# Final norm of an encoder moved into the feed-forward loop, and one GpSimd memset moved later

## The reference

```
out1 = _layernorm(x + attn_out, ln1_g, ln1_b)
h = jax.nn.elu(out1 @ W1 + b1)
ffn_out = h @ W2 + b2
return _layernorm(out1 + ffn_out, ln2_g, ln2_b)      # rsqrt(var + 1e-6) * g + b
```

## Time and profile before

| what | us |
|---|---|
| median of 3 runs | 2630.42 |
| lowest and highest | 2629.88, 2640.3 |
| the profiled execution | 2632.62 |
| its span in the profile | 2630.4 |

### The profile page before, as it was taken

The page is one execution under the profiler, slowest core; times in us unless marked ns, Lnnn a source line. Parts: engine busy times, 40 slices in busy tenths (PEclk is TensorE's granted clock), DMA queues, the critical chain, the costliest instruction groups (busy, mean ns, idle before and its releaser), DMA issues. The chain is left out here.

```text
span 2630.4 us, 95467 instructions
## 1 busy us (share of the span) xinstructions
PE 2416.6 (92%) x39473; PEld 2073.5 (79%) x39473; DVE 1644.4 (63%) x3145; ACT 1457.2 (55%) x4096; POOL 1051.6 (40%) x1152
## 2 busy tenths in 40 slices
PE   6899999999989999997579998999999989899999
PEld 5788888888867888885479986777777778788888
DVE  4566666666667777675655554777777757544553
ACT  3555555555566676664644443777777734422222
POOL 2343344333440000002344444666666623355555
PEclk8999999999999999998869998999999989799999
DMA  5544333334333111110020000200010010065463
GB/s 199 213 152 144 144 144 144 144 144 148 118 150 148 48 40 48 40 40 2 3 69 1 0 0 19 54 26 28 24 30 24 19 53 0 2 139 116 107 134 76
DMA packets 60306, 206.08 MB, mean 78 GB/s; under 512 B 6670, under 2 KB 20498, under 8 KB 51226
## 3 DMA queue, kind: packets, MB, share of 16 engines
q1 hardware_dynamic: 60188, 204.41, 24.5%
HBM read 182.88 MB, written 21.51 MB: 78 GB/s over the span
## 5 line engine op out<-in xcount | busy, mean ns | idle before, releaser
L558 POOL TENSOR_TENSOR l_pn<-l_probs,l_rden 128x1024 f32<-128x1024 f32 x128 | 242.9, 1898 | 454.1 <-DVE l_rden L400 454.1
L494 ACT ACTIVATE l_probs<-ps,l_nmax 128x257 f32<-128x257 f32 x512 | 236.3, 474 | 272.4 <-DVE l_nmax L394 270.2
L959 POOL TENSOR_TENSOR l_probs<-l_probs,l_rden 128x1024 f32<-128x1024 f32 x128 | 242.5, 1895 | 170.5 <-DVE l_rden L810 170.5
L895 ACT ACTIVATE l_probs<-ps,l_nmax 128x257 f32<-128x257 f32 x512 | 236.3, 474 | 59.7 <-DVE l_nmax L804 59.7
L394 DVE TENSOR_REDUCE l_nmax<-ps 128x2 f32<-128x514 f32 x256 | 165.4, 688 | 164.3 <-PE ps L286 164.3
L286 PE MATMUL ps<-l_ctxQ,l_q 32*128 32x257 f32 x3072 | 205.2, 396 | 40.5 <-ACT l_q L501 27.2
L2714 POOL TENSOR_TENSOR m_hh<-m_hh,m_cb 128x512 f32<-128x512 f32 (+1 forms) x136 | 179.7, 1322 | 141.6 <-DVE m_hh L2666 134.4
L804 DVE TENSOR_REDUCE l_nmax<-ps 128x2 f32<-128x514 f32 x256 | 165.4, 688 | 61.1 <-PE ps L696 57.5
L2570 ACT ACTIVATE m_sg<-ps 128x512 f32<-128x512 f32 (+1 forms) x136 | 81.5, 599 | 219.7 <-PE ps L111 218.8
L286 PEld LDWEIGHTS ps<-l_ctxQ,l_q 32*128 32x128 f32 x3072 | 148.6, 186 | 69.0 <-issue 30.7
L2666 DVE TENSOR_TENSOR m_hh<-ps,m_sg 128x512 f32<-128x512 f32 (+1 forms) x136 | 93.9, 690 | 167.6 <-PE ps L111 151.7
(11 more groups left out here) (373 smaller groups left out, 6429.4 us busy)
## 6 DMA issues: line engine op xcount, KB each, us to landing
l_ctxQ<-in_ctx_q SPq DMA_DIRECT2D x32, 1542.0 KB, 6.4
l_ctxK<-in_ctx_k SPq DMA_DIRECT2D x16, 1536.0 KB, 6.4
l_early<-in_ctx_k SPq DMA_DIRECT2D x16, 1536.0 KB
enc_dash<-kept SPq DMA_DIRECT2D x32, 512.0 KB, 3.2
m_cb<-combined SPq DMA_DIRECT2D x32, 512.0 KB, 10.7
l_ctxT<-in_ctx_t SPq DMA_DIRECT2D x32, 385.5 KB, 3.3
m_cb<-combined SPq DMA_DIRECT2D x16, 768.0 KB, 16.6
kept<-enc_va SPq DMA_DIRECT2D x10, 512.0 KB, 2.7
```

Of the source, the lines that this page charges most:

```text
L494: nc.scalar.activation(probs[:, par % 2, hg, :], ps[:, S_B + hg, 0:NK], ACT.Exp, bias=nmax[:, par, hg:hg + 1], accum_out=den[:, par, hg:hg ...
L558: nc.gpsimd.tensor_tensor(pn[:, b % 2, :, :], probs[:, b % 2, :, 0:NK - 1], rden[:, b, :, None].to_broadcast([P, HG, NK - 1]), ALU.mult).t ...
L895: nc.scalar.activation(probs[:, b, hg, :], ps[:, S_B + hg, 0:NK], ACT.Exp, bias=nmax[:, b, hg:hg + 1], accum_out=den[:, b, hg:hg + 1]).the ...
L959: nc.gpsimd.tensor_tensor(pr, pr, rden[:, b, :, None].to_broadcast([P, HG, K_W]), ALU.mult).then_inc(norm_ok, 1)
```

## The change

The block of the final norm is gone. Its work stands in the feed-forward loop, group by group: VectorE computes the variances of a group right after its statistics (`variances`), GpSimd takes them to the power -0.5 and makes the shift (`roots`), ScalarE normalises in the next turn (`final`), GpSimd multiplies by the gain and adds to `k.x` (`added`), and VectorE takes the statistics of x another turn later (`count_x`). The loop has two turns more for it. In the expert stage GpSimd's memset stands behind its eight casts instead of ahead of them.

```diff
             def groups(step):
-                for g in range(NG + 1):
+                for g in range(NG + 3):
                     step(g, g % 2, lambda d: 0 <= g + d < NG)
...
                     for n in range(PART):
                         t = PART * g + n
-                        nc.vector.bn_stats(at(k.stats, t), at(res, t))
+                        last = nc.vector.bn_stats(at(k.stats, t), at(res, t))
+                    last.then_inc(c_ok, 1)
+
+                def variances(g):
+                    ts = slice(PART * g, PART * g + PART)
+                    col = lambda n: k.stats[:, ts, n:n + 1].rearrange("p t o -> p (t o)")
+                    dve.wait_ge(c_ok, g + 1)
+                    if g:
+                        dve.wait_ge(var_ok, g)
+                    nc.vector.tensor_tensor(part[:, 0, :], col(1), col(4), ALU.add)
+                    nc.vector.tensor_tensor(part[:, 1, :], col(1), col(4), ALU.subtract)
+                    nc.vector.tensor_tensor(part[:, 2, :], col(2), col(5), ALU.add).then_inc(p_ok, 1)
+                    dve.wait_ge(p_ok, 2 * g + 1)
+                    nc.vector.tensor_scalar(f_mean[:, ts], part[:, 0, :], -0.5, None, ALU.mult)
+                    nc.vector.tensor_tensor(part[:, 3, :], part[:, 1, :], part[:, 1, :], ALU.mult)
+                    nc.vector.tensor_scalar(part[:, 4, :], part[:, 2, :], 1.0 / D, EPS_ENC, ALU.mult, ALU.add
+                                            ).then_inc(p_ok, 1)
+                    dve.wait_ge(p_ok, 2 * g + 2)
+                    nc.vector.scalar_tensor_tensor(f_var[:, ts], part[:, 3, :], 0.25, part[:, 4, :], ALU.mult, ALU.add
+                                                   ).then_inc(var_ok, 1)
+
+                def count_x(g):
+                    dve.wait_ge(x_ok, g + 1)
+                    nc.vector.nop(nofuse=True)
+                    for n in range(PART):
+                        t = PART * g + n
+                        nc.vector.bn_stats(at(k.stats, t), at(k.x, t))
...
                     if has(-1):
                         result(g - 1, 1 - j)
                         count(g - 1)
+                        variances(g - 1)
+                    if has(-3):
+                        count_x(g - 3)
...
+                def final(g, j):
+                    act.wait_ge(f_ok, g + 1)
+                    if g > 1:
+                        act.wait_ge(x_ok, g - 1)
+                    for n in range(PART):
+                        t = PART * g + n
+                        last = nc.scalar.activation(f4[:, j, n, :], res[:, t, :], ACT.Identity, bias=f_shift[:, t:t + 1],
+                                                    scale=f_rstd[:, t:t + 1])
+                    last.then_inc(fa_ok, 1)
...
                         for c in (2, 3):
                             expo(g, c, True)
+                    if has(-2):
+                        final(g - 2, j)
...
-                        nc.gpsimd.tensor_tensor(xs, xs, rows[:, 4:5, :].to_broadcast(wide), ALU.add)
-
+                        nc.gpsimd.tensor_tensor(xs, xs, rows[:, 4:5, :].to_broadcast(wide), ALU.add).then_inc(xb_ok, 1)
+                    if has(-1):
+                        roots(g - 1)
+                    if has(-2):
+                        added(g - 2, j)
+
+                def roots(g):
+                    ts = slice(PART * g, PART * g + PART)
+                    pool.wait_ge(var_ok, g + 1)
+                    nc.gpsimd.tensor_tensor(f_rstd[:, ts], f_var[:, ts], neg_half[:, :], ALU.pow).then_inc(root_ok, 1)
+                    pool.wait_ge(root_ok, g + 1)
+                    nc.gpsimd.tensor_tensor(f_shift[:, ts], f_mean[:, ts], f_rstd[:, ts], ALU.mult).then_inc(f_ok, 1)
+
+                def added(g, j):
+                    pool.wait_ge(fa_ok, g + 1)
+                    n, xs = f4[:, j, :, :], part_of(k.x, g)
+                    nc.gpsimd.tensor_tensor(n, n, rows[:, 3:4, :].to_broadcast(wide), ALU.mult).then_inc(g_ok, 1)
+                    pool.wait_ge(g_ok, g + 1)
+                    pool.wait_ge(xb_ok, g + 1)
+                    nc.gpsimd.tensor_tensor(xs, n, xs, ALU.add).then_inc(x_ok, 1)
...
-        with ExitStack() as end:
-            sem = lambda n: k.sem(f"fin_{n}")
...
-            @block.scalar
-            def _(act):
-                rstd_act(nc, k, act, ln)
...
-            nc.gpsimd.memset(next_ones, 1.0).then_inc(row_ok, 1)
-            pool.wait_ge(row_ok, 1)
             nc.gpsimd.memset(one[:, :], 1.0).then_inc(one_ok, 1)
...
             for g in range(NG):
                 high(g)
+            pool.wait_ge(xh_ok, NG)
+            nc.gpsimd.memset(next_ones, 1.0).then_inc(row_ok, 1)
+            pool.wait_ge(row_ok, 1)
```

More of the change, by code:

```diff
@@ L1448, in stage_performer @@
             hT = sb("hT", [P, 2, NF, 512])
+            f4, neg_half, part = sb("f4", [P, 2, PART, D]), sb("neg_half", [P, PART]), sb("part", [P, 5, PART])
+            f_mean, f_var, f_rstd, f_shift = [sb(n, [P, T]) for n in ("f_mean", "f_var", "f_rstd", "f_shift")]
+            c_ok, xb_ok, half_set, p_ok, var_ok, root_ok, f_ok, fa_ok, g_ok, x_ok = [sem(n) for n in (
+                "c_ok xb_ok half_set p_ok var_ok root_ok f_ok fa_ok g_ok x_ok").split()]
             (ln, w_mm, set_ok, n_ok, tr_mm, tr_ok, up_mm, low_ok, m_ok, h_ok, y_mm, y_ok, base_ok, sum_ok) = [sem(n) for n in (
@@ L1627, in step @@
                         nc.gpsimd.tensor_tensor(r, r, row[:, None, :].to_broadcast(wide), ALU.add).then_inc(base_ok, 1)
-                        nc.gpsimd.tensor_tensor(xs, xs, rows[:, 4:5, :].to_broadcast(wide), ALU.add)
-                groups(step)
-        with ExitStack() as end:
-            sem = lambda n: k.sem(f"fin_{n}")
-            PART = 4
-            NG = T // PART
-            n4 = end.enter_context(nc.sbuf_tensor("fin_n4", [P, 2, PART, D], F32))
-            shift = end.enter_context(nc.sbuf_tensor("fin_shift", [P, T], F32))
-            ln, sh_ok, n_ok, g_ok, x_ok = sem("ln"), sem("sh_ok"), sem("n_ok"), sem("g_ok"), sem("x_ok")
-            block = end.enter_context(nc.Block())
-            @block.scalar
-            def _(act):
-                rstd_act(nc, k, act, ln)
-                act.wait_ge(sh_ok, 1)
-                for g in range(NG):
-                    if g > 1:
-                        act.wait_ge(x_ok, g - 1)
-                    for n in range(PART):
-                        t = PART * g + n
-                        last = nc.scalar.activation(n4[:, g % 2, n, :], res[:, t, :], ACT.Identity, bias=shift[:, t:t + 1],
-                                                    scale=k.rstd[:, t:t + 1])
-                    last.then_inc(n_ok, 1)
-            @block.gpsimd
-            def _(pool):
-                for g in range(NG):
-                    pool.wait_ge(n_ok, g + 1)
-                    n = n4[:, g % 2, :, :]
-                    nc.gpsimd.tensor_tensor(n, n, rows[:, 3:4, :].to_broadcast([P, PART, D]), ALU.mult).then_inc(g_ok, 1)
-            @block.vector
-            def _(dve):
-                rstd_dve(nc, k, dve, ln, EPS_ENC)
-                nc.vector.scalar_tensor_tensor(shift[:, :], k.mean[:, :], -1.0, k.rstd[:, :], ALU.mult,
-                                               ALU.mult).then_inc(sh_ok, 1)
-                for g in range(NG):
-                    dve.wait_ge(g_ok, g + 1)
-                    xs = k.x[:, PART * g:PART * g + PART, :]
-                    nc.vector.tensor_tensor(xs, n4[:, g % 2, :, :], xs, ALU.add).then_inc(x_ok, 1)
-                    dve.wait_ge(x_ok, g + 1)
-                    for n in range(PART):
-                        t = PART * g + n
-                        nc.vector.bn_stats(k.stats[:, t, :], k.x[:, t, :])
@@ new lines, in added @@
+                def added(g, j):
[5 more added lines that the diff above has]
+                    nc.gpsimd.tensor_tensor(xs, n, xs, ALU.add).then_inc(x_ok, 1)
+                nc.gpsimd.memset(neg_half[:, :], -0.5).then_inc(half_set, 1)
@@ L1677, in keep_clock @@
+                pool.wait_ge(half_set, 1)
+                groups(step)
 def keep_clock(nc, k, bank, n):
```

## The result

The changed kernel takes 2643.49 us (median of 17 runs) against 2632.43 of the kernel before (17 runs taken with them): ratio 1.0039, 95% interval 1.003 to 1.0048. By the ratio it is slower by 10.3 us (7.9 to 12.6). The forecast was +8.5. The profiled execution took 2643.49 us with a span of 2641.2; that of before had 2630.4.

The account below looks back on a forecast made before the run. The prediction took TensorE to bound the feed-forward loop, with the final norm wholly on the path behind it. Loop +19.0, end -10.9 and expert stage +0.4 gave +8.5 us, 2638.9 us on the median, range 2628 to 2654.

Parts of the forecast that it names:

- the power: GpSimd's power -0.5 in the roots: no row to size it, taken as 0.7 us, between 0.20 and 2.4.
- The ring: Feed-forward loop: VectorE and GpSimd wait for each other in a circle, making a turn 12.45 us instead of 7.44.
- p: Time of one GpSimd power, put at 0.7 us; each us of it moves the whole time 8 us.
- stall: VectorE's normalisations held beside a GpSimd instruction: one of 1.2 us, making 2.2 us with 1.1 alone, less overlap.
- Number of turns: Loop results 1 to 4: the first after 9.85 us, the next three at the long turn of 12.45 each.
- Results 5 to 7: Last three loop results: 6.4 us by VectorE's own work, 8.1 by TensorE's turn plus stalls, then 5.6.
- rival C: Feed-forward loop: TensorE's clock falls to half after idle time and stays down, about +16, 2655 us; chance 0.08.
- Tail: From last result to end of last statistics: 11.1 us instead of 22.0, a gain of 10.9.
- Expert stage: Start of the expert stage: root 1.5 us sooner, but the moved memset delays GpSimd's chain and a softmax copy; +0.4 us.
- Rival A: GpSimd keeps its lead, the loop its 7.44 us a turn, only the end counts: 2619.9 us; chance 0.10.
- B: GpSimd's power is dear, 1.5 us or more; at 2.4 the kernel takes 2652.5 us; chance 0.20.
- D: GpSimd's first power, in turn 1, loads code on the path, 6.6 us: 2645.5 us in all; chance 0.04.

Follow-up runs that it names:

- e1: The changed kernel with GpSimd making the base of group g+1 in turn g, ahead of the roots of group g-1; ratio to before 1.0007.
- e2: The changed kernel with GpSimd's power -0.5 made a multiply of the same shape, leaving out the root of the variance; ratio to before 1.002.
- e3: The changed kernel with 16 useless TensorE products ahead of its wait for the transposes of groups 5 to 7; ratio to before 1.002.
- e12: The changed kernel with base a turn ahead, bias adds in the attention block, normalisations behind statistics, memset behind weights, transposes behind the fourth up product; ratio 0.9976.
- e10: The changed kernel with base a turn ahead, memset behind weights and inputs, and VectorE's normalisations behind its statistics; ratio to before 1.0008.
- e5: The changed kernel with GpSimd's adds of the last bias to x moved from the turns to the loop's start; ratio to before 1.0048.

## Why the prediction was right

The time, the sign and the mechanism came as forecast, +8.5 against a local +8.94 and a whole +10.3. That a turn came out within 0.05 us is in part luck: the power was sized 0.32 too low and the other terms 0.37 too high. Step by step:

- **The ring** is there with every term. In the turn shown: variances 0.85 (predicted 1.0), roots 1.33 (p + 0.36), `added` and base 5.21 (5.2), wait and normalisations up to the next elu 2.0 (2.2), elu to variances 3.01 (3.0). Sum 12.40. e1 shows the cause: with the lead given back, the loss is gone.
- **The power** was chosen at 0.7 and is 1.02, the one term sized too low; the formula gives 12.77 with it and 12.40 was measured, since variances and stall were 0.15 and 0.2 shorter. With the power as it is and the other terms as they were put, the forecast would have been 2.6 us higher. The price per us of p is as said (e2: 0.82 less, 0.82 a turn, and 7.0 us of the stretch for the 6.6 of eight powers).
- **Number of turns**: 9.85, 3 x 12.45 predicted, 9.82, 12.39, 12.4, 12.4 measured.
- **Results 5 to 7** were given 6.4, 8.1, 5.6 and took 9.42, 7.01, 4.60. Here the clock, rival C, had its share: behind 3.75 us of idle time TensorE ran at 1.2 GHz for most of 7.6 us. The sum of the three is 21.0 for the 20.1 predicted; e3 has 6.63, 7.79, 5.32, nearly the forecast. So the forecast's sum had nothing for the clock there, and results 6 and 7 hid half of that.
- **Tail**: 11.1 and 11.08. **Expert stage**: +0.4 and +0.15, by the mechanism told, the copy at 2.44. One row there was misread: L2049 ended at 1346.66 as the third L2126 began (1346.5), not the second (1344.0); the step built on it, the copy inside the third one, holds.
- **Rival A** (the lead stays, -10.5) would have needed the base before the second elu; VectorE waited 2.73 to 5.33 us for it. **B** was nearer than thought: 1.02 lies between the chosen 0.7 and the 1.5 from which it counts. **D** is false: the first power, at 1241.26, took 1.02 us as the seven others did, it started 0.07 behind the end of the variance it waits for, and the instruction behind it came 0.08 later. Had the 6 us of the Trainium skill (GPSIMD Engine Reference, Instruction dispatch) applied here, result 1 would have come that much later than 9.82.

What the prediction didn't see is that the lead alone doesn't make the change pay. It priced GpSimd's chain as harmless if only off the ring ("five times 1.25, 0.2 and p are 7.2, less than 7.44"); with the measured 1.02 the sum is 7.47 already, and the stall of the normalisations was not in it. e1 has the base off the ring, at turns of up to 10.4: rival A, as it was priced, could not have come by the queue's order alone; it took e12's other moves to reach turns near 7.44. The chances have a slip too: "slower by more" was given 0.31, and B, C and D alone add up to 0.32. The remaining 1.4 us between +8.94 and +10.3 lie within the ratio's interval; no run puts them down to the change.

## What to carry to other kernels

When work is added to an in-order queue, ask which instruction behind it used to run ahead of its reader: an engine that is idle half of the time has nothing to give if its lead is lost, and a wait put ahead of early work can turn two queues into a ring whose length is the sum of what both do on it. Put early work ahead of the new wait, put VectorE's SBUF-to-SBUF work where GpSimd waits, and then look for the next reader of what has become late (here the transposes). A move that makes a start sooner (the memset) is worth something only if what it delays is not met later in the same stage.

## What the runs showed of the hardware

- GpSimd's power with two SBUF operands takes 1.02 us on 128x4, in all eight places within 5 ns, where the multiply of that shape takes 0.20 (e2). That is 0.8 us more for four columns; the first use was not dearer.
- A chain of GpSimd instructions with no gap passes about one of VectorE's SBUF-to-SBUF normalisations at each border: 4.60 us for four in e1, 1.10 in e10 with GpSimd idle. The elu, with one operand in PSUM (the memory that TensorE writes its products to), went on beside such a chain at full rate: in the kernel after two from 1264.09 took 1.39 us beside L1684 and L1689, as two took 1.41 in the kernel before.
- Which of VectorE's instructions are held depends on GpSimd's. Beside the memset of the kernel before, L75 to L77 (two SBUF inputs) kept their 0.13 to 0.20 us and L79 (one input) took 1.99; beside e5's adds, L75 took 1.28. The timeline of the kernel before:

```profile
1313.01 0.13 DVE L75 TENSOR_TENSOR half<-stats 128x32 f32<-128x32 f32 x1
1313.06 0.20 DVE L76 TENSOR_TENSOR half<-stats 128x32 f32<-128x32 f32 x1
```

The Trainium skill (SBUF — State Buffer, SBUF: two separate sides) states this difference: an instruction of VectorE with two SBUF inputs shuts out, and is shut out by, only a GpSimd operation that reads SBUF. Both rows agree: the memset reads nothing and left L75 at 0.13, e5's adds read x and L75 took 1.28.

- TensorE's clock was at 0.55 over 7.6 us behind 3.75 us of idle time, mostly at 1.2 GHz; in the turn of result 3 it fell to 0.51 behind 3.74 us and was back at 1.00 over the 5.03 us of work from 1264.47. Beside the slack of the loop the fall ahead of result 5 cost 1.25 us (e3).
